# The output bias of the last experts: by VectorE's passes, or as a product of TensorE

## What is computed

```python
x = x + _L0_gnn_ref(_layernorm(x), ...)
x = x + _L0_ffn_ref(_layernorm(x), ...)
x = x + _L1_gnn_ref(_layernorm(x), ...)       # two attention layers over the edges
x = x + _L1_ffn_ref(_layernorm(x), ...)

def _L1_ffn_ref(x, ...):                      # NUM_EXPERTS, TOP_K, HEADS = 4, 2, 4
    h = (x @ W_gat).reshape(M, HEADS, NUM_EXPERTS)
    ...                                       # softmax over each node's incoming edges, sums of h[src]
    scores = _layernorm(agg, ...).reshape(M, HEADS, NUM_EXPERTS).mean(1)
    topk_s, topk_i = jax.lax.top_k(scores, TOP_K)
    w = jax.nn.softmax(topk_s, axis=-1)
    out = jnp.zeros_like(x)
    for ei in range(NUM_EXPERTS):
        g = jnp.where(topk_i == ei, w, 0.0).sum(-1)
        hh = jax.nn.gelu(x @ W1[ei] + b1[ei], approximate=False)
        out = out + g[..., None] * (hh @ W2[ei] + b2[ei])
    return out
```

## Time and profile before

| | us |
|---|---|
| median of 3 runs | 8212.54 |
| lowest and highest | 8207.43, 8218.19 |
| the profiled execution, its time | 8239.37 |
| the profiled execution, its span | 8237.6 |
| third edge stage, with dense steps | 6273 to 7968 of the span |
| last stage | 8019 to 8238 of the span |

### The profile page before, as it was taken

How to read it: one execution, slowest core, us unless ns; L and a number is a source line. 1 busy time by engine, 2 the same in 40 slices (tenths; PEclk the granted TensorE clock), 3 DMA queues, 4 the chain that set the end, 5 groups by cost and what they waited for, 6 DMA issues and landing times. The chain is left out here.

```text
span 8237.6 us, 111355 instructions
## 1 busy us (share of the span) xinstructions
PE 5031.7 (61%) x22610; PEld 2967.0 (36%) x22610; DVE 5393.4 (65%) x18770; ACT 3619.7 (44%) x11436; POOL 5680.1 (69%) x5781
## 2 busy tenths in 40 slices
PE   0000008905289983577776577777326898988988
PEld 0000008802145552344444344444212444444435
DVE  9999308903222224677777677887526888888887
ACT  0000004401122221677776377777315777677762
POOL 2777777777677777777777777777766666666650
PEclk9999999956699996899999799998666767677669
DMA  6111112200010001334343244444111111111113
GB/s 160 26 24 26 24 22 47 45 3 2 2 29 2 2 2 36 94 106 108 107 108 96 66 108 108 108 108 107 44 5 38 24 24 25 23 24 25 24 30 116
DMA packets 476333, 427.34 MB, mean 52 GB/s; under 512 B 269726, under 2 KB 409876, under 8 KB 475668
## 3 DMA queue, kind: packets, MB, share of 16 engines
q0 software_dynamic: 214016, 282.62, 14.9%
q1 hardware_dynamic: 224020, 120.13, 5.4%
q10 hardware_dynamic: 37632, 17.48, 0.9%
HBM read 341.50 MB, written 78.72 MB: 51 GB/s over the span
## 5 line engine op out<-in xcount | busy, mean ns | idle before, releaser
L436 POOL DMA_INDIRECT pay_sorted<-pay,pos x1856 | 1890.9, 1019 | 698.0 <-issue 572.7
L770 POOL DMA_INDIRECT G<-tab_gat,pay x1856 | 1791.0, 965 | 592.4 <-issue 551.7
L770 POOL DMA_INDIRECT G<-tab_rt,pay x1216 | 1152.5, 948 | 627.7 <-PE pLU L847 327.7
L274 POOL DMA_INDIRECT attr_sorted<-rows,pos x832 | 843.2, 1013 | 389.3 <-issue 253.4
L844 PE MATMUL pU<-G,PM 128*128 128x257 f32 x3712 | 1060.0, 412 | 1.3 <-DVE acc L1155 1.3
L790 PE MATMUL pA<-identb,G 128*20 128x128 bf16 (+1 forms) x3072 | 425.8, 244 | 675.7 <-DMA G<-tab_gat,pay 571.6
L1058 DVE TENSOR_REDUCE mt<-pW 128x4 f32<-128x2048 f32 x304 | 695.4, 2287 | 165.6 <-PE pW L808 165.2
L889 ACT ACTIVATE aT<-pA 20x256 bf16<-20x256 bf16 (+1 forms) x1232 | 520.4, 422 | 630.3 <-PE pA L790 623.9
L844 PEld LDWEIGHTS pU<-G,PM 128*128 128x128 f32 x3712 | 696.3, 209 | 66.7 <-ACT PM L941 1.2
L790 PEld LDWEIGHTS pA<-identb,G 128*20 128x20 bf16 (+1 forms) x3072 | 178.9, 98 | 1251.3 <-DMA G<-tab_gat,pay 955.9
L322 ACT ACTIVATE rows<-lo 128x16 f32<-128x16 f32 x52 | 11.6, 229 | 1140.2 <-DMA attr_sorted<-rows,pos 1080.8
(11 more groups left out here) (323 smaller groups left out, 11369.4 us busy)
## 6 DMA issues: line engine op xcount, KB each, us to landing
pay_sorted<-pay,pos POOLq DMA_INDIRECT x1856, 2.1
G<-tab_gat,pay POOLq DMA_INDIRECT x1856
G<-tab_rt,pay POOLq DMA_INDIRECT x1216, 2.4
expert_parts<-pos SPq DMA_DIRECT2D x144, 128.0 KB, 1.7
yl<-expert_parts SPq DMA_DIRECT2D x36, 512.0 KB, 4.0
attr_sorted<-zattr SPq DMA_DIRECT2D x1, 16896.0 KB, 53.2
rows<-attr_sorted ACTq DMA_DIRECT2D x256, 66.0 KB
attr_sorted<-rows,pos POOLq DMA_INDIRECT x832, 2.2
```

Source lines behind the costliest of these rows:

```text
L274: pool.indirect_dma_start(out=self.attr_sorted, out_offset=bass.IndirectOffsetOnAxis(ap=pos0[:, t:t + 1], axis=0), in_=rows[:, j, k, :], i ...
L436: pool.indirect_dma_start(out=out, out_offset=bass.IndirectOffsetOnAxis(ap=self.pos[g][:, lo + n:lo + n + 1], axis=0), in_=self.pay[g][:, ...
L770: pool.indirect_dma_start(out=G[:, j, k, 0:R], out_offset=None, in_=table, in_offset=bass.IndirectOffsetOnAxis(ap=pay[:, g % (2 * PART), k ...
```

## The change

In both stages the bias goes into the accumulation of the output product: after the four products of a block comes a fifth, of a row of 128 ones (`self.ones[0:1, :]`) with the bias row of the expert (256 columns), which closes the accumulation group. B2 becomes a tensor of one partition. In the edge stage it lies in an unused piece of `wide[1]` and its load is a tenth one after the nine of L744. In the last stage its load has a semaphore of its own, for which TensorE waits before the first output; VectorE's setup waits for three loads in place of four. `with_bias` and its semaphore are gone, and `add` waits for the load or the drain of its part itself.

```diff
+            B2 = wide[1][0:1, 4 * K * P:4 * K * P + NX1 * D].bitcast(F32).rearrange("p (e d) -> p e d", e=NX1)
+            loads = dense["loads"] + [(B2, self.i["L1_ffn_b2"].rearrange("(a e) d -> a e d", a=1))]
...
-                    for to, what in dense["loads"]:
+                    for to, what in loads:
...
-                    pe.wait_ge(s_xw, 16 * len(dense["loads"]))
+                    pe.wait_ge(s_xw, 16 * len(loads))
...
                     for k in range(HID // P):
-                        ins = nc.tensor.matmul(pE[:, 0:D], hid[u % 2][:, k, i * P:(i + 1) * P], W2[:, x, k, :],
-                                               start=(k == 0), stop=(k == HID // P - 1))
+                        nc.tensor.matmul(pE[:, 0:D], hid[u % 2][:, k, i * P:(i + 1) * P], W2[:, x, k, :],
+                                         start=(k == 0), stop=False)
+                    ins = nc.tensor.matmul(pE[:, 0:D], self.ones[0:1, :], B2[0:1, x, :], start=False, stop=True)
...
-        B2 = sb("B2", [P, E, D])
+        B2 = sb("B2", [1, E, D])
...
-            sp.dma_start(B2[:, :, :], i_["L1_ffn_b2"].rearrange("e (a d) -> a e d", a=1).partition_broadcast(P)
-                         .rearrange("q a e d -> q (a e) d")).then_inc(s_w, 16)
+            sp.dma_start(B2[:, :, :], i_["L1_ffn_b2"].rearrange("(a e) d -> a e d", a=1)).then_inc(s_b2, 16)
...
+                if u == 0:
+                    pe.wait_ge(s_b2, 16)
...
                     for q in range(MT):
-                        ins = nc.tensor.matmul(pO[u % 2][:, n, :], hid[u % 2][:, q, n * P:(n + 1) * P], W2[:, e, q, :],
-                                               start=(q == 0), stop=(q == MT - 1))
+                        nc.tensor.matmul(pO[u % 2][:, n, :], hid[u % 2][:, q, n * P:(n + 1) * P], W2[:, e, q, :],
+                                         start=(q == 0), stop=False)
+                    ins = nc.tensor.matmul(pO[u % 2][:, n, :], self.ones[0:1, :], B2[0:1, e, :], start=False, stop=True)
...
-            dve.wait_ge(s_w, 64)
+            dve.wait_ge(s_w, 48)
...
-                t = part(todo[n])
-                v.tensor_tensor(t, t, B2[:, e, :].unsqueeze(1).to_broadcast([P, blocks(cc), D]), ALU.add).then_inc(s_t, 1)
-
-            def add(n):
-                cc, e = todo[n]
-                t = part(todo[n])
-                dve.wait_ge(s_t, n + 1)
                 if n:
                     dve.wait_ge(s_y, n)
...
-            with_bias(0)
             for n in range(len(todo)):
-                nxt = n + 1 < len(todo)
-                if nxt:
-                    with_bias(n + 1)
                 add(n)
```

More of the change, by code:

```diff
@@ L968, in dense_drain @@
                     if n == 0:
-                        act.wait_ge(s_xw, 16 * len(dense["loads"]))
+                        act.wait_ge(s_xw, 16 * len(loads))
                     x = u % NX1
@@ L1989, in last_experts @@
         s_w, s_c, s_v, s_s, s_x, s_e = (sem(x) for x in ("s_w", "s_scores", "s_var", "s_std", "s_for_exp", "s_exp"))
-        s_h, s_hc, s_o, s_od, s_t, s_y, s_out = (sem(x) for x in (
-            "s_h", "s_hc", "s_o", "s_od", "s_t", "s_y", "s_out"))
+        s_b2, s_h, s_hc, s_o, s_od, s_y, s_out = (sem(x) for x in (
+            "s_b2", "s_h", "s_hc", "s_o", "s_od", "s_y", "s_out"))
         s_yl = [sem(f"s_yloaded{n}") for n in range(RY)]
@@ L2157, in part, with add @@
                 return yr[left.index(unit) % SLOTS][:, 0:n, :]
-            def with_bias(n):
+            def add(n):
                 cc, e = todo[n]
+                t = part(todo[n])
                 if cc < PRE:
```

## The result

The changed kernel is slower: 8249.17 us median of 7 runs (8231.16 to 8258.33) against 8207.43 us for the kernel before (7 runs, 8190.27 to 8220.26); the ratio is 1.0049, 95% interval 1.0034 to 1.0065, which is +40 us. The forecast was 33 us faster.

What follows compares the result with a forecast made beforehand. TensorE was taken to bound the last stage and low-clock edge iterations, VectorE the high-clock ones. Terms +62 - 98 + 0 + 3 = -33 us against the profiled execution, 8179 us on the median; eight-in-ten range 8100 to 8250 us.

Steps and rivals of the forecast that it cites:

- So I take the price of the full-height product: Both stages: each one-row bias product costs what a 128-row one does, 0.43 us at full clock, 0.86 at half.
- What they give if all of their time ran as the stretches between them do: Edge stage: nine low-clock stretches of 41 to 92 us break up, worth 122 us; four fifths taken, -98 us.
- Last stage: After the edge stage: 52 bias products delay TensorE's end by 22.5 us, dropped VectorE passes shorten the end; net +3 us.
- low is not short: Reading of edge-stage rows: four products of 28 rows take some 0.24 us each, so fewer rows save no time.
- The tail: Last stage, VectorE's additions after the last full part: 24.6 us without bias passes, plus 1 us waiting for loads.
- Edge stage, the added time: Edge stage: 72 output iterations at low clock grow by 0.86 us each, +62 us; at high clock the product hides.
- Edge stage, the rhythm: Edge stage: unequal iterations break up the long low-clock stretches, -98 us; none over 40 us, mean clock 0.76 or more.
- Rhythm as a cause: Edge stage: equal iterations of 6.78 us, with heavy fp32 products in the same place, hold the clock down, not lack of work.
- A: Rival, edge stage: low stretches stay as the rhythm locks in again; +65 us, 8278 us, slower; chance 0.17.
- f: Edge stage: share of the long low stretches that dissolves; whole change is 65 - 122 f us, forecast 0.66 to 1.
- C: Rival, edge stage: every iteration takes 5.43 us, -130 + 40 us; whole change -87 us, 8125 us; chance 0.20 including beyond forecast.
- The rule weighed in the prediction: Edge stage: skill says sustained work releases the throttle; this would give the whole 122 us; rejected as contradicting the trace.

## Why the prediction was wrong

Two steps failed. The first is "So I take the price of the full-height product": a one-row product among full-height ones costs 0.81 us and not 0.43. The second, and the larger in us, is "What they give if all of their time ran as the stretches between them do", with the -98 us taken from it: the long low stretches did break up, and the low time hardly shrank.

- *Last stage.* Forecast TensorE +22.5 us and the stage +3; measured +42.6 and +25.0. The price is 0.81 us, not 0.43; the bound of 45 us had it, and I took the value by the full-height row. The row that I used for "low is not short" (28 rows, 0.24 us) was four products of one height after each other: it priced the columns, and none of my rows priced a change of height among fp32 products without a gap. The tail was 29.2 us against my 25.6: it waits 4.4 us for loads, which took 4.7 us to land (median) in place of 4.0. These 22 us are a third of the miss. With full height the stage's chain came out at 204.5 us, 22.7 over before.
- *Edge stage, the added time.* Forecast 0.86 us for a low output iteration, measured 1.02, the same error. The number of such iterations was off the other way. Counted from one L806 to the next, the clock is low for 252 us in output iterations, 460 before, so the price falls on some 252/7.79 = 32 of them and not on 72: an estimate of +33 us in place of +62. At the high level it hid, as forecast.
- *Edge stage, the rhythm.* The forecast asked for no stretch at 0.50 over 40 us and a mean clock of 0.76. The first came true: by the clock records of the trace no low spell is longer than 20.5 us, apart from the one in which the dense steps begin, where before had eleven of over 27.5 us, 638 us together. But spells like this one come again and again, 27 of 20.5 us, with a stretch after each in which the clock goes back and forth; the third row is both together, the fourth all of the dense steps:
```profile
6472.20:6492.70 20.50, 6.79 (x3) 0.50 0.17 30
...
6492.70:6520.20 27.50, 24.46 (x128) 12.44 (x128) 25.23 (x110) 20.94 (x58) 19.62 (x22) 0.87 0.15 22
...
6472.20:6520.00 47.80, 43.65 (x192) 21.09 (x192) 39.60 (x169) 34.20 (x100) 30.11 (x33) 0.71 0.16 25
6255.80:7954.80 1699.00, 1552.49 (x6900) 745.28 (x6899) 1420.20 (x6047) 1233.17 (x3560) 1094.94 (x1157) 0.73 0.14 24
```
  Within the dense steps the low time went from 992 to 926 us, and more of it lies in hidden iterations (680 us, 537 before). The prediction had the broken stretches run at 0.84. For the stage: forecast -36 us, measured +9 (mean of 1774, 1768 and 1758 us in three kernels with the one-row product, against 1768, 1760 and 1747 without; the two groups overlap, so +9 is uncertain). With the +33 us above, the rhythm gave some 24 us back and not 98, an estimate. The edge stage is the other two thirds of the miss.
- *Rhythm as a cause.* Low spells of over 27.5 us within the dense steps stand in the three traces without an added product there and in none with one (the spell in which the steps begin left out); what makes them long is not shown. That the low time comes from them fell: with one row they are gone and the clock is 0.72, with 64 and 128 rows in the same places it is 0.78 and 0.81. With a full-height product in every step the steps were to be even again, and the clock is 0.90. What the clock follows in these kernels is the height of the added products and their number; a busy TensorE is not enough.
- *The rivals.* The outcome lies in A (f under 0.40; its number is +65 us), and part of that is luck. A's long stretches did not stay, and its 62 us for the edge stage did not come. But its argument, that the rhythm may lock in again at another phase, is nearest to what the trace shows, the spells of 20.5 us. C's stage, -130 + 40 = -90 us, is what a full-height product gave: 1674.5, 1662.7 and 1680.0 us against a mean of 1758, -86.
- *The rule weighed in the prediction.* The Trainium skill ("TensorE: Matmul & The Clock Gate", section "What's actually happening") has activity release the throttle. Busy time as the profile shows it is not that activity: 95% busy with the clock at 0.65 in one kernel, 85% busy with 0.90 in its full-height twin. By the rule an added product could only raise the clock; full-height ones did (0.81 to 0.94), and one row in every step lowered it.

## What to carry to other kernels

Adding a bias as a product of a row of ones spares VectorE its passes, and is dear on TensorE when it stands among full-height fp32 products: here 0.81 us for 256 columns in place of 0.43, each time. Pad it to 128 rows (with zeros too, as far as the edge stage shows), or group such products so that the height changes seldom. And where TensorE runs without a gap at the low clock, ask what height its products have: in this kernel one more product of full height in every second step made the stage 78 to 96 us shorter, and one in every step, useless ones among them, 114 to 141 us. Where TensorE has room for it at the high clock, it is worth a trial.

## What the runs showed of the hardware

- In these traces a weight load of 1 or 64 rows does not run ahead beside full-height products, nor a full-height one beside it: 0.33 us idle at each change, 0.19 us added twice. With 128 rows there is none. The Trainium skill ("TensorE: Matmul & The Clock Gate", section "The mechanism") states that loads overlap running products only when their row groups differ, and also that a load into the background weight buffer is pulled ahead. The first, taken alone, does not agree with the trace: loads of equal, full height overlap.
- The mean granted clock of the edge stage, one profiled execution for each kernel, followed the height of 144 products: 0.72 with 1 row, 0.78 with 64, 0.81 with 128; 0.90 with 288 of full height, 0.94 with 576, 0.65 with 288 of one row. Zeros in the rows made no difference (0.81). Without an added product it was 0.70, 0.70 and 0.71. How the chip counts this is left open.
